# Attention on Trainium2: from scores computed twice to softmax on the score rows, with the probabilities turned by TensorE

## What is computed

```python
# attention, for 8 batches and 16 heads of 32 columns
Q = rope(proj(layernorm(x), W_q)); K = rope(proj(ctx, W_k)); V = proj(ctx, W_v)
scores = einsum('bhqd,bhkd->bhqk', Q, K) / sqrt(32)       # 224 queries x 750 keys a head
scores = where(mask == 0, -inf, scores)
attn = softmax(scores, axis=-1)
x = x + tanh(g_xattn) * (einsum('bhqk,bhkd->bhqd', attn, V) @ W_o.T)
# experts: softmax of 8 logits over layernorm(x), 56 rows per expert and batch by top_k
x = x + tanh(g_ffn) * scatter(gating * expert(gather(layernorm(x))))
```

## Time and profile before

| | |
|---|---|
| runs | 1953.86 us median of 3 (1951.43 to 1954.47) |
| profiled execution | 1952.03 us, span 1950.1 us |
| busy in the span | PE 1816.3 us (93%), DVE 1020.4 (52%), ACT 717.0 (37%), POOL 213.3 (11%) |
| mean granted TensorE clock | 0.970 of full speed |
| DMA | 257.33 MB, 132 GB/s on average |
| chain that ended last | PE 49% of the span, DMA, DVE, POOL and ACT under 1% each |

### The profile page before, as it was taken

How to read it: one execution, slowest core, us unless ns; L and a number is a source line. 1 busy time by engine, 2 the same in 40 slices (tenths; PEclk the granted TensorE clock), 3 DMA queues, 4 the chain that set the end, 5 groups by cost and what they waited for, 6 DMA issues and landing times. The chain is left out here.

```text
span 1950.1 us, 30053 instructions
## 1 busy us (share of the span) xinstructions
PE 1816.3 (93%) x11654; PEld 1564.5 (80%) x11654; DVE 1020.4 (52%) x1650; ACT 717.0 (37%) x1134; POOL 213.3 (11%) x288
## 2 busy tenths in 40 slices
PE   7999974999999999998299999999999999999995
PEld 6989962776676676775189999999999999999995
DVE  6665643676676576574444353543535445354441
ACT  3232221444344444353044343433424334343340
POOL 0000001112122112111100020200202011020101
PEclk9999996999999999999689999999999999999998
DMA  5545446565465564551333353533535334353431
GB/s 221 192 172 204 159 151 159 135 166 140 123 171 139 125 177 134 128 152 39 113 105 109 98 147 116 137 108 99 154 108 137 114 108 136 108 145 108 120 105 19
DMA packets 77229, 257.33 MB, mean 132 GB/s; under 512 B 10824, under 2 KB 10824, under 8 KB 75856
## 3 DMA queue, kind: packets, MB, share of 16 engines
q1 hardware_dynamic: 65136, 221.92, 37.1%
q0 software_dynamic: 12000, 34.13, 7.4%
HBM read 193.39 MB, written 51.61 MB: 126 GB/s over the span
## 5 line engine op out<-in xcount | busy, mean ns | idle before, releaser
L1413 PE MATMUL gu_ps<-xs_hi,ws_hi 128*128 128x448 f32 x1024 | 372.4, 364 | 3.0 <-DVE xs_lo L1348 3.0
L1415 PE MATMUL gu_ps<-xs_hi,ws_lo 128*128 128x448 f32 x1024 | 371.9, 363 | 0.0
L1414 PE MATMUL gu_ps<-xs_lo,ws_hi 128*128 128x448 f32 x1024 | 371.0, 362 | 0.0
L786 DVE CUSTOM_DVE_ANT_0 junk<-m_ps,mq 112x752 f32<-112x752 f32 x256 | 236.1, 935 | 198.0 <-PE m_ps L1047 195.7
L1343 DVE TENSOR_TENSOR ws_lo<-w_raw,ws_hi 128x1024 fp32r<-128x1024 f32 x192 | 235.4, 1226 | 189.1 <-ACT ws_hi L1293 188.1
L671 ACT ACTIVATE e_t<-s_ps 125x448 f32<-125x448 f32 x384 | 201.1, 547 | 221.7 <-PE s_ps L1074 221.1
L1293 ACT ACTIVATE ws_hi<-w_raw 128x1024 fp32r<-128x1024 f32 x192 | 201.7, 1051 | 164.4 <-PE y_ps L1432 146.6
L1413 PEld LDWEIGHTS gu_ps<-xs_hi,ws_hi 128*128 128x128 f32 x1024 | 192.7, 188 | 15.4 <-issue 3.3
L1414 PEld LDWEIGHTS gu_ps<-xs_lo,ws_hi 128*128 128x128 f32 x1024 | 192.6, 188 | 13.5
L1415 PEld LDWEIGHTS gu_ps<-xs_hi,ws_lo 128*128 128x128 f32 x1024 | 192.8, 188 | 13.2
L1074 PE MATMUL s_ps<-qs,ks 128*125 128x224 f32 x768 | 197.8, 353 | 0.0
(11 more groups left out here) (133 smaller groups left out, 2552.0 us busy)
## 6 DMA issues: line engine op xcount, KB each, us to landing
w_raw<-wstream SPq DMA_DIRECT2D x192, 512.0 KB, 3.5
ks<-k_split SPq DMA_DIRECT2D x192, 188.0 KB, 3.8
k_split<-k_split SPq DMA_DIRECT2D x32, 752.0 KB, 3.5
v_rows<-v_out SPq DMA_DIRECT2D x16, 750.0 KB
vs<-v_rows SPq DMA_DIRECT2D x16, 750.0 KB
c_raw<-ctxT SPq DMA_DIRECT2D x7, 1500.0 KB, 12.9
qs<-q_hi POOLq DMA_DIRECT2D x64, 112.0 KB, 3.0
mq_raw<-maskq SPq DMA_DIRECT2D x8, 656.2 KB, 10.3
```

Source lines behind the costliest of these rows:

```text
L786: nc.vector.tensor_tensor_reduce(junk[u % 2][:].rearrange("p (a n) -> p a n", a=2), m_ps[u % 2][0:QP, :, 0:KN], mq[:, qc].rearrange("p (a ...
L1413: nc.tensor.matmul(o, w_hi[s][:, w], xs_hi[:, c], start=(c == 0), stop=False)
L1414: nc.tensor.matmul(o, w_hi[s][:, w], xs_lo[:, c], start=False, stop=False)
L1415: mm = nc.tensor.matmul(o, w_lo[s][:, w], xs_hi[:, c], start=False, stop=(c == DC - 1))
```

## The change

The scores are computed once. DVE's pass over the rows now keeps what it used to throw away: it writes the masked scores, times -1/sqrt(32), to `sm` in SBUF, and the minimum of each row to `least`. ACT exponentiates these rows (112 x 752, two per head, scale -1, bias from `least`) and has the sums of the rows accumulated by the same call. PE turns the probabilities, 12 transposes of 112 x 125 per head into three tiles `t_ps` of 125 x 448. Each tile is copied to `e_t`: tiles 0 and 2 by ACT, tile 1 of every head by DVE.

The matmuls with ones, the second computation of the scores, the transposed mask with its load and its pass on DVE, the selector rows and the transposed maxima are gone. The inverse sums take another way: DVE inverts 112 x 8 sums per four heads, POOL spreads each to 32 columns, PE turns them (`turn_parts`, into the other half of `o_ps`), ACT copies them (`copy_parts`), and DVE multiplies (`normalise`). The values of four heads are 24 matmuls in three parts, in the turns t with t % 4 not 0. The row scores run MLEAD = 3 heads ahead of the turn, before 5. The change also restates a few waits and moves `flags`, `stack_q` and `x_columns` by a turn.

```diff
+SR = 4
+MLEAD = 3
+VPART = KC // (HG - 1)
+DVE_TILE = 1
+DVE_SLOTS = tuple(range(H))
...
-        junk = [sb(st, f"junk{j}", [QP, SK]) for j in range(2)]
-        mx = sb(st, "mx", [QP, 2, QC, P])
+        sm = sb(st, "sm", [QP, SR, QC, SK])
+        least, sums = sb(st, "least", [QP, KSLOTS, QC]), sb(st, "sums", [QP, 2, QC, HG])
+        parts, spread = sb(st, "parts", [QP, 2, QC * HG]), sb(st, "spread", [QP, 2, QC, P])
         e_t = [sb(st, f"e_t{j}", [KP, KC // 2, PAIR]) for j in range(2 * HG)]
-        c_vs, cx = sb(st, "c_vs", [P, 2, PAIR]), sb(st, "cx", [P, NG, S])
+        c_r, cx = sb(st, "c_r", [P, S]), sb(st, "cx", [P, NG, S])
...
-        s_ps = [ps(st, f"s_ps{j}", [P, 512]) for j in range(2)]
+        m_ps = [ps(st, f"m_ps{j}", [P, 2, 512]) for j in range(QC)]
+        t_ps = [ps(st, f"t_ps{j}", [P, 512]) for j in range(2)]
...
+        def tile_of(b, h, pc):
+            return NT * b + KC // 2 * h + pc
+        def on_dve(h, pc):
+            return pc == DVE_TILE and h in DVE_SLOTS
+        def emptied(n):
+            b, h, pc = n // NT, n % NT // (KC // 2), n % (KC // 2)
+            dve = len(DVE_SLOTS) * b + sum(on_dve(k, DVE_TILE) for k in range(h)) + (pc >= DVE_TILE and on_dve(h, DVE_TILE))
+            return (t_dve, dve) if on_dve(h, pc) else (t_act, n + 1 - dve)
...
-                    hold(s_made, NST * b + KC // 2 * (h + 2 - KSLOTS))
+                    hold(m_made, NS * b + QC * (h + 2 - KSLOTS))
...
-                        if t == 0 and not last:
-                            load_mt(b + 1)
...
-                def normalise(b, q):
-                    hold(recip_done, NG * b + q + 1)
-                    nc.gpsimd.tensor_tensor(cx[:, q], c_vs[:, q % 2, 0:S], cx[:, q], ALU.mult).then_inc(cx_done, 1)
+                def spread_parts(b, q):
+                    hold(parts_done, NG * b + q + 1)
+                    hold(r_made, NG * b + q - 1)
+                    nc.gpsimd.tensor_copy(spread[:, q % 2].rearrange("p c (r d) -> p (c r) d", r=HG),
+                                          parts[:, q % 2, :, None].broadcast_to((QP, QC * HG, DK))).then_inc(spread_done, 1)
...
+                        if t % HG == HG - 1:
+                            spread_parts(b, t // HG)
...
+                def exp(b, h, qc):
+                    act.wait_ge(masked[qc], H * b + h + 1)
+                    if h % HG == 0:
+                        after(act, parts_done, NG * b + h // HG - 1)
+                    rows = sm[:, h % SR, qc]
+                    nc.scalar.activation(rows, rows, ACT.Exp, bias=least[:, h % KSLOTS, qc:qc + 1], scale=-1.0,
+                                         accum_out=sums[:, h // HG % 2, qc, h % HG:h % HG + 1]).then_inc(exp_done[qc], 1)
+                def empty(b, h, pc):
+                    act.wait_ge(t_made, tile_of(b, h, pc) + 1)
                     if h % HG == 0 and pc == 0:
                         after(act, pv_done, NG * b + h // HG - 1)
...
+                    nc.scalar.activation(e_t[h % (2 * HG)][:, pc], t_ps[tile_of(b, h, pc) % 2][0:KP, 0:PAIR], ACT.Copy).then_inc(t_act, 1)
+                def copy_parts(b, q):
+                    act.wait_ge(r_made, NG * b + q + 1)
+                    nc.scalar.activation(c_r[:], o_ps[:, S:PAIR], ACT.Copy).then_inc(r_copied, 1)
...
+                        def next_exp(qc):
+                            if t + 1 < H:
+                                exp(b, t + 1, qc)
+                            elif not last:
+                                exp(b + 1, 0, qc)
                         for pc in range(KC // 2):
...
+                            if not on_dve(t, pc):
+                                empty(b, t, pc)
+                            if pc < QC:
+                                next_exp(pc)
+                            if pc == 0 and t % HG == 1:
+                                if t > HG:
+                                    copy_parts(b, t // HG - 1)
                                 elif not first:
...
+                                    copy_parts(b - 1, NG - 1)
+                            if pc == 0 and t in (1, 2) and not last:
+                                x_columns(b + 1, t - 1)
+                            if pc == 0 and t in (12, 13) and not first:
                                 x2_columns(b - 1, t - 12)
-                            if t == 15:
-                                logit_exp(b - 1)
+                        if t == 8 and not last:
+                            high_q(b + 1)
+                        if t == 15 and not first:
+                            logit_exp(b - 1)
...
+                def mask_scores(b, h, qc):
                     if h == 0:
                         dve.wait_ge(mq_done, b + 1)
...
+                    dve.wait_ge(m_made, NS * b + QC * h + qc + 1)
+                    hold(t_made, tile_of(b, h - SR, KC // 2 - 1) + 1)
+                    nc.vector.tensor_tensor_reduce(sm[:, h % SR, qc].rearrange("p (a n) -> p a n", a=2), m_ps[qc][0:QP, :, 0:KN],
+                                                   mq[:, qc].rearrange("p (a n) -> p a n", a=2), -SCALE, 3e38, ALU.add, ALU.min,
+                                                   least[:, h % KSLOTS, qc:qc + 1]).then_inc(masked[qc], 1)
+                def empty(b, h, pc):
+                    dve.wait_ge(t_made, tile_of(b, h, pc) + 1)
+                    if h % HG == 0:
+                        after(dve, pv_done, NG * b + h // HG - 1)
+                    nc.vector.tensor_copy(e_t[h % (2 * HG)][:, pc], t_ps[tile_of(b, h, pc) % 2][0:KP, 0:PAIR]).then_inc(t_dve, 1)
+                def invert(b, q):
                     for qc in range(QC):
...
+                        dve.wait_ge(exp_done[qc], H * b + HG * q + HG)
+                    after(dve, spread_done, NG * b + q - 1)
+                    nc.vector.reciprocal(parts[:, q % 2], sums[:, q % 2].rearrange("p c r -> p (c r)")).then_inc(parts_done, 1)
+                def normalise(b, q):
+                    dve.wait_ge(pv_done, NG * b + q + 1)
+                    dve.wait_ge(r_copied, NG * b + q + 1)
                     if q == 0:
                         after(dve, rest_made, R_USES * (b - 1) + R_Y + QC)
-                    nc.vector.reciprocal(cx[:, q], c_vs[:, q % 2, S:PAIR]).then_inc(recip_done, 1)
+                    nc.vector.tensor_tensor(cx[:, q], o_ps[:, 0:S], c_r[:], ALU.mult).then_inc(cx_done, 1)
...
+                        for qc in range(QC):
+                            if t + MLEAD < H:
+                                mask_scores(b, t + MLEAD, qc)
+                            elif not last:
+                                mask_scores(b + 1, t + MLEAD - H, qc)
+                            if qc == 0 and on_dve(t, DVE_TILE):
+                                empty(b, t, DVE_TILE)
+                        if t % HG == 0:
+                            if t >= 2 * HG:
+                                normalise(b, t // HG - 2)
+                            elif not first:
+                                normalise(b - 1, t // HG + 2)
+                        if t % HG == HG - 1:
+                            invert(b, t // HG)
...
+                def turn_rows(b, h, pc):
+                    if pc == 0:
+                        for qc in range(QC):
+                            pe.wait_ge(exp_done[qc], H * b + h + 1)
+                    n = tile_of(b, h, pc)
+                    if n >= 2:
+                        pe.wait_ge(*emptied(n - 2))
                     for k in range(2):
                         c = 2 * pc + k
-                        mm = nc.tensor.matmul(o[:, k * S:k * S + S], ks[:, h % KSLOTS, c * KP:c * KP + KP], qs[:, h, :],
-                                              start=False, stop=(k == 1))
-                    mm.then_inc(s_made, 1)
+                        for qc in range(QC):
+                            a = k * S + qc * QP
+                            mm = nc.tensor.transpose(t_ps[n % 2][0:KP, a:a + QP], sm[:, h % SR, qc, c * KP:c * KP + KP], ident[0:QP, 0:QP])
+                    mm.then_inc(t_made, 1)
+                def turn_parts(b, q):
+                    after(pe, cx_done, NG * b + q)
+                    pe.wait_ge(spread_done, NG * b + q + 1)
+                    for qc in range(QC):
+                        mm = nc.tensor.transpose(o_ps[:, S + qc * QP:S + qc * QP + QP], spread[:, q % 2, qc], ident[0:QP, 0:QP])
+                    mm.then_inc(r_made, 1)
...
...
+                        pe.wait_ge(r_copied, NG * b + q + 1)
+                        for pc in range(KC // 2):
+                            pe.wait_ge(*emptied(tile_of(b, HG * q + HG - 1, pc)))
+                            others = [r for r in range(HG - 1) if on_dve(HG * q + r, pc)]
+                            if others:
+                                pe.wait_ge(*emptied(tile_of(b, HG * q + others[-1], pc)))
+                    for c in range(VPART * part, VPART * part + VPART):
                         for r in range(HG):
                             h = HG * q + r
```

(45 more changed lines are left out.)

242 lines of the change are left out of this document (49 added, 193 removed).

## The result

The changed kernel takes **1998.14 us** (median of four runs, 1997.96 to 2001.40), the kernel before 1952.64 (1950.43 to 1954.47): ratio 1.0237, 95% interval 1.0220 to 1.0255, 45.5 us slower. The forecast was 1972, slower by 20: the sign is right, the size is less than half of what came, and the time lies in the range (1926 to 2008). The profiled execution took 1997.96, with a span of 1996.1 (before 1950.1).

What follows compares the result with a forecast made beforehand. PE was taken to bound attention, but its savings were to be lost to waits on DVE and ACT: 1952.0 + 19 (attention) - 10.6 (lead-in) + 2 (half clock there) + 10 (clock falls) = 1972 us, range 1926 to 2008.

Steps and rivals of the forecast that it cites:

- PE's work at full clock: Attention: PE's time per batch falls from 74.2 to 59.5 us after work removed and added.
- PE's waits: Attention: waits on DVE and ACT, turn by turn in a middle batch, sum to 17.9 us.
- half clock: Attention: the 5 us wait in turn 0 drops PE's clock, about 1.7 us lost, six times, +10.
- The bound that I gave this term: PE's new transposes: four may take 0.31 instead of 0.37 us; total effect of this bound alone -9 us.
- Shorter waits (up to 2.6) I cost at nothing: Attention: waits other than turn 0's 5 us were priced with no loss of clock; a rival covered them.
- The rival of the low clock: Attention: clock stays low after turn 0's wait, 1989 us, or in ten turns of 16, over 2100; chance 12%.
- the 0.7 of the plain turns: Turns 3 and 14: ACT's loop makes a turn 3.1 us, not 2.78, losing 0.33 in each.
- The 0.64 and the 0.15 in the loop through ACT: ACT's 3.1 us loop: 0.64 for transposes done and seen, 0.15 for end and wake-up.
- 19 + 2 + 10 = 31: Attention stage: +19 us from longer batches, +2 from half clock in the lead-in, +10 from clock falls.
- The lead-in: Before attention: PE's first turn starts at 334.9, 10.6 us earlier; removed loads not on the path.
- ACT's exp: Each 112 x 752 exp on ACT: pitch 0.93 us, between 0.74 and 1.13.
- DVE is not late: Attention: DVE's work fits between its passes, turn 0 waits 1.8 us, no clock fall, 1924 us; chance 18%.

Runs made afterwards that it cites:

- run 8: Run 7's kernel with DVE's turned tile given to ACT in turns 0, 9, 10 and 15: 1897.72 us, ratio 0.9722.
- run 10: Run 7's kernel with no turned tile on DVE at all, ACT copying them: 1916.92 us, ratio 0.9816.
- run 9: Run 1's kernel with 11 extra unused matmuls filling PE's wait in turn 0 of batches 1 to 6: 1947.55 us, ratio 0.9974.
- run 6: Changed kernel with both reorderings, normalise ahead of DVE's passes and POOL's root ahead of spread_parts: 1934.84 us, ratio 0.9920.
- run 2: Changed kernel with only POOL's root put ahead of spread_parts in turn 15: 1999.68 us, ratio 1.0246.
- run 12: Run 8's kernel with POOL's root put back behind spread_parts: 1916.29 us, ratio 0.9811.
- run 1: Changed kernel with DVE's normalise ahead of its passes in turns 0, 4, 8 and 12: 1945.74 us, ratio 0.9963.
- run 5: Changed kernel with all three turned tiles of a head copied by ACT, none by DVE: 1959.12 us, ratio 1.0031.
- run 11: Run 8's kernel with normalise put back behind DVE's two passes: 1966.14 us, ratio 1.0065.
- run 7: Run 6's kernel with ACT's copy_parts ahead of the exp in turns 1, 5, 9 and 13: 1915.52 us, ratio 0.9814.
- run 3: Changed kernel with 11 extra unused matmuls filling PE's wait in turn 0 of batches 1 to 6: 1995.18 us, ratio 1.0221.
- run 4: Changed kernel with 44 unused transposes filling PE's wait in turn 0 of batches 1 to 6: 1997.98 us, ratio 1.0227.

## Why the prediction was right in sign and wrong in size

By its own steps, us per middle batch (after: five batches; the work at full clock is that of runs 8 and 10, which make the same matmuls at clock 1.00):

| step | forecast | measured |
| --- | --- | --- |
| PE's work at full clock | 59.5, less the 2.3 of waits in it: 57.2 | 64.7 |
| PE's waits | 17.9, with these 2.3: 20.2 | 12.8 |
| half clock | 1.7 | 81.85 - 12.8 - 64.7 = 4.4 |
| period | 79.1 | 81.9 |

- **The base of the sum** held waits that I took for work. The 59.5 starts from the whole period of the kernel before, 74.2, and in that PE waits 2.3 us a batch. Its waits from 471.72 to 842.99, five batches:

```profile
PE w_ps L1013 <- DVE x_res L833: 6.7, 5, 1.3
PE m_ps L1058 <- DVE mx L786: 4.6, 5, 1.2
```

- **The work of PE** was the first mis-sized term, by 7.5. I priced four transposes at 0.37 wherever they stand and the values at 16/24 of 1.28. A turn of the new kernel changes between the kinds of work more often, and by the rows from 595.73 to 602.22 the last transposes of each of 16 turns take 0.16 more, the scores ahead of values 0.10 and the values 0.04 more in 12 turns: 2.6 + 1.7 = 4.3. Added up from start to start over run 8's five batches, without recorded waits, a batch has 21.5 of transposes (17.8 forecast), 14.5 of scores (12.9 before), 10.7 of values (10.2), 7.0 of output projection (6.6 before), 2.1 of turned x (1.4 before) and 1.3 of turned sums (1.0). The second scores, taken off with 22.1, were 21.8. That is the whole 7.5. The bound that I gave this term pointed the wrong way only (0.31, less work).
- **The falls of the clock** were the second, and here a sentence of the prediction failed as a statement: "Shorter waits (up to 2.6) I cost at nothing". Behind the waits of 1.6 to 1.7 us in turns 8 and 12 the clock falls as it does in turn 0. By the 1.7 of the earlier trace rows once a batch I had 10 us; 4.4 a batch is 26 over six. The price of one (1.7) was nearly right (2.0 in run 9, and 4.4 over 2.6 falls is 1.7), their number was not. The rival of the low clock named this mechanism, but with ten turns kept down; two or three are.
- **The waits** for `normalise` were in the right places: turn 0 4.4 to 4.9 (5.05 forecast), turn 4 1.95 (2.2), turn 8 1.68 (1.8), turn 12 1.64 (2.6). Their source was right too: DVE begins its passes 4.4 us into turn 0 (559.50 to 563.88, 4.3 forecast), with 1.76 for root (1.6). The other waits were priced too high: `copy_parts` 1.1 a batch recorded (3.6), the late tile of turn 15 0.7 in four batches of the five (1.1), that of turn 10 (0.85) and the 0.7 of the plain turns not at all. Part of the reason lies in the first step: PE's own part of turn 0 ahead of the turned sums lasts 2.2 (559.50 to 561.70) and not 1.93, so that PE comes later to the wait. The rest wasn't taken apart. So an error of 7.5 in the work and one of 7.4 in the waits cancel. That is luck, and what is left of the difference is the clock.
- The 0.64 and the 0.15 in the loop through ACT come from no row. From the start of PE's transposes to ACT's copy of them the trace after has 0.69 (559.50 to 560.19).
- Over the attention stage, from the first query projection to the last output projection, it took 628.0 against 570.9, 57.1 more, where the sum had 19 + 2 + 10 = 31. Six middle batches at 2.85 above forecast are 17 of these 26; the other 9 lie in the first and the last batch with the tail and weren't taken apart further.
- **The lead-in** came out right by luck, by a way that the text had wrong. The timeline of PE after:

```profile
322.77 1.59 PE L1012 MATMUL m_ps<-ks,qs 96*112 96x376 f32 x4 [9.89 <-DMA qs<-q_lo]
...
328.55 1.02 PE L1028 MATMUL t_ps<-cst,sm 112*125 112x112 f32 x4
...
342.84 0.65 PE L967 MATMUL w_ps<-xT,wq_sb 128*128 128x224 f32 x2
```

  The first scores wait for the rotated query rows, which land 6.1 us sooner than before (322.77 against 328.83), so "The loads removed are not on the path" fails as a statement. DVE had these rows ready no sooner (318.24 against 317.80, the end of `low_q`), so it was the transfers: their low part's median from issue to landing is 3.0 us after and 9.9 before. Of the loads issued between 288 and 318, the transposed mask's (at 294.76) is the only one that is gone, which makes it the likeliest; no run tested it. The first transposes came at 328.55, not 334.9. What was gained there went again in turns 0 and 1, to half clock and to waits of 1.66 for `xn` and 0.82 for the late tile. The first query projection is 10.4 earlier than before's 353.23, against 10.6 forecast.
- **ACT's exp** was about right. It is 0.91 long, its accumulator read 0.19, and the pitch 0.91 against 0.93:

```profile
560.63 0.91 ACT L638 ACTIVATE sm<-sm,least 112x752 f32<-112x752 f32 x1
561.45 0.19 ACT L638 ACTIVATION_READ_ACCUMULATOR sm<-sm,least 112x1 f32 x1
561.54 0.91 ACT L638 ACTIVATE sm<-sm,least 112x752 f32<-112x752 f32 x1
```

- The rival "DVE is not late" (1924) didn't happen, because of the order that the forecast named. Its content is borne out in part by run 6, which puts `normalise` and `root` early and lands at 1935.

## What to carry to other kernels

Taking work off the engine that bounded this kernel paid only once the short steps by which the others hand on to it stood early in their written order. PE's work fell by 7.3 us a batch (72.0 to 64.7, waits left out), and the period rose by 7.6. Moving one multiply of 0.4 us took 6.6 off again, and moving it, a root, a copy and four tiles made the same change 2.8% faster than the kernel before. Price a wait with the clock that it costs afterwards, and a mixed sequence of matmuls by rows that show the same changes of kind. When one such fault is cured and nothing is gained, cure them together before judging it: root first was worth nothing in run 2, 11 us in run 6 and 19 in run 12.

## What the runs showed of the hardware that was not expected

- With a wait of 2.4 us or more in turn 0, TensorE's clock fell to half during it or soon behind it, in all five traced batches of the changed kernel and of runs 1, 2, 5, 11 and 12. Waits of 1.6 to 2.0 had a fall behind them in some turns and none in others: in the changed kernel turn 8 in five batches of five, turn 12 in four, turn 4 in none. Three of 0.7 to 0.8 soon after one another had one in three batches of five (run 6) and in one of three (run 7). The half clock then mostly lasted 3 to 7 us, and one fall costs about 2.0 us of the period (run 9).
- Shortening or filling one wait (runs 2, 3, 4) left the time within 3 us, since the falls behind the other waits stayed, grew longer, or came at new places: with the one in turn 0 gone, turn 4 had one.
- 41 recorded transposes in 4.1 us kept the clock at 1.00, as 22 matmuls did.
- One matmul of 32-bit floats, 128 x 224, stands in the trace as two, 4.34 us for 11.
- A kind of work on PE costs more ahead of another kind: transposes 0.36 ahead of scores and 0.53 at the end of a turn, scores 0.41 ahead of transposes and 0.51 ahead of values.
